# Fused vision-transformer tower on one core: biases as stacked products in PSUM sums, a shorter last norm, gate bias products in four pieces, and a new order on every engine

## The reference, cut to what matters

```python
h = concat([cls_token, patches @ W.T + b]) + pos_enc
# layer 0: norm, gated recurrence over the 37 tokens, residuals; then the feed-forward part
z = sigmoid(norm(x) @ Wg.T + bg); c = norm(x) @ Wc.T + bc      # h_t = (1 - z_t) h_(t-1) + z_t c_t
h = gelu(x @ absmean(W_fc)); h = layernorm(h, ln_w, ln_b) @ absmean(W_proj).T
# layer 1: attention of one head with rotary positions and a causal mask; then a ternary projection
Q, K = rope(x @ Wq.T + bq), rope(x @ Wk.T + bk);  V = x @ Wv.T + bv
A = softmax(where(causal, Q @ K.T / sqrt(256), -inf));  attn = (A @ V) @ Wf.T + bf
y = clip(round(norm(x) / s), -127, 127) @ (ternary_weight - 1).T * s + bias     # s = max(act_scale, 1e-5)
```

## Time and profile before

| what | us |
|---|---|
| median of 3 runs | 170.02 |
| lowest, highest | 169.44, 171.18 |
| the profiled execution's own time | 171.55 |
| its span, first to last instruction | 169.5 |
| PE busy in the span | 151.0 (89%) |
| DVE busy | 128.4 (76%) |
| ACT busy | 96.2 (57%) |
| POOL busy | 93.5 (55%) |

### The profile page before, as it was taken

One profiled execution on the slowest core, in us unless ns is written; L12 is line 12 of the kernel. 1 busy time (PEld: TensorE's weight loads), 2 busy tenths in 40 slices (PEclk: granted clock), 3 DMA queues, 4 the chain that ended last, 5 costly groups with the idle time before them and its releaser, 6 DMA issues.

```text
span 169.5 us, 3258 instructions
## 1 busy us (share of the span) xinstructions
PE 151.0 (89%) x933; PEld 125.1 (74%) x933; DVE 128.4 (76%) x400; ACT 96.2 (57%) x235; POOL 93.5 (55%) x193
## 2 busy tenths in 40 slices
PE   0898999999999899899999999999999996997442
PEld 0668788899997774578987989999988973764231
DVE  0036065979899899799788989879798888648893
ACT  3104087279245798998879669555644461666400
POOL 0001342053521757108986598788778897587850
PEclk9999699999999999999999999999999998799855
DMA  5999991000500000000101011110200000001213
GB/s 183 255 411 420 421 385 52 0 2 0 155 4 0 0 4 0 2 4 0 41 24 31 0 37 31 33 35 0 62 0 0 0 4 0 4 2 31 81 60 118
DMA packets 6614, 12.26 MB, mean 72 GB/s; under 512 B 1061, under 2 KB 4165, under 8 KB 6341
## 3 DMA queue, kind: packets, MB, share of 16 engines
q1 hardware_dynamic: 6597, 12.05, 20.5%
HBM read 9.66 MB, written 1.21 MB: 64 GB/s over the span
## 4 chain that ended last, share of the span: by engine, by line
PE 58%; DVE 12%; POOL 11%; issue 7%; DMA 4%; ACT 3%; SPq 3%; DVEq 0%; POOLq 0%
PE bank L519 30%; PE bank L639 12%; POOL small L1464 5%; DMA w_gate<-w_gate_in 4%; PE bank L711 4%; PE bank L651 3%; PE bank L779 3%; SPq L461 3%; POOL small L1468 2%; DVE q L1430 2%; PE bank L796 1%; PE bank L816 1%; POOL end L1574 1%; POOL small L1459 1%; DVE end L1436 1%
## 5 line engine op out<-in xcount | busy, mean ns | idle before, releaser
L1459 POOL TENSOR_SCALAR small<-small 128x1 f32<-128x1 f32 (+3 forms) x48 | 11.5, 240 | 52.4 <-DVE small L1065 49.8
L639 PE MATMUL bank<-w_tok,x_raw 128*128 128x256 f32 x108 | 29.0, 426 | 5.3 <-DMA w_tok<-w_tok_in 4.9
L1464 POOL TENSOR_TENSOR small<-small,powers 128x1 f32<-128x1 f32 (+4 forms) x48 | 30.9, 645 | 4.7 <-DVE small L1330 1.5
L639 PEld LDWEIGHTS bank<-w_tok,x_raw 128*128 128x128 f32 x108 | 22.6, 216 | 9.0 <-issue 4.9
L519 PE MATMUL bank<-pj,gt_hi 128*128 128x256 f32 x72 | 18.4, 294 | 0.0
L519 PE MATMUL bank<-pj,gt_lo 128*128 128x256 f32 x72 | 17.5, 282 | 0.0
L1384 DVE SCALAR_TENSOR_TENSOR rope<-bank,packed,consts 128x324 f32<-128x324 f32 (+2 forms) x24 | 13.1, 610 | 1.2 <-PE bank L519 1.0
L519 PE MATMUL bank<-fc,n1t_hi 128*128 128x512 f16 x36 | 13.6, 378 | 0.4 <-ACT g L964 0.3
L519 PEld LDWEIGHTS bank<-pj,gt_hi 128*128 128x128 f32 x72 | 13.5, 188 | 0.4
L519 PEld LDWEIGHTS bank<-pj,gt_lo 128*128 128x128 f32 x72 | 13.6, 189 | 0.1
L519 PE MATMUL bank<-fc,n1t_lo 128*128 128x512 f16 x36 | 13.6, 379 | 0.0
(11 more groups left out here) (178 smaller groups left out, 434.8 us busy)
## 6 DMA issues: line engine op xcount, KB each, us to landing
x_raw<-x_in SPq DMA_DIRECT2D x9, 384.0 KB, 7.7
out_dram<-end SPq DMA_DIRECT2D x10, 108.0 KB
w_fc<-w_fc_in SPq DMA_DIRECT2D x1, 1024.0 KB, 9.9
w_pj<-w_pj_in SPq DMA_DIRECT2D x1, 1024.0 KB, 12.7
w_tok<-w_tok_in SPq DMA_DIRECT2D x2, 384.0 KB, 4.1
w_gate<-w_gate_in SPq DMA_DIRECT2D x1, 512.0 KB, 7.4
w_qk<-w_qk_in SPq DMA_DIRECT2D x1, 512.0 KB, 12.5
ln_w<-ln_w_in SPq DMA_DIRECT2D x1, 512.0 KB, 3.7
```

Of the source, the lines that this page charges most:

```text
L639: mm(out[:, 0:D], x_raw[:, i, k, :], w_tok[:, k, :], start=(k == 0), stop=False)
L1459: return nc.gpsimd.tensor_scalar(small[0:n, i, out:out + 1], small[0:n, i, value:value + 1], factor, add, ALU.mult, ALU.add)
L1464: return gt(small[0:n, i, r:r + width], small[0:n, i, ve:ve + width], powers[0:n, 0:width], ALU.pow)
```

## The change

- Keys and values: the class key moves from column 0 of each group's keys to the last, the mask follows (a second mask for the group of 2 images). The transposed probabilities then have the class as their last row, and the class's value is row n of `value`: each `value` sum opens with one product on all 128 rows (a 1 in rows 64 and 96 of `sel`, 0 elsewhere, by `away`, which now holds class value + bias, high and low part) that writes it there. `attend` multiplies n + 1 rows. POOL's 11 `vbias` steps go; DVE's `attend` waits for the DMA of the residual instead.
- `c_value`: DVE adds the bias first (`c_bias`), ACT copies 128 rows, DVE makes two low parts; `c_row` takes one product more, and DVE only copies it.
- Output bias: bias / s, high part in row 0 and low part in row 32 (`w_out_shift`, one ACT and one DVE instruction), enters each `out` sum as a first product on 64 rows, issued ahead of the wait for the copied transposes. POOL's 12 `biased` steps go, and DVE's wait for them.
- Last norm: s squared enters the variance step, so that the power gives 1/(s * deviation) at once; POOL's L1564 goes, and L1459 reads its factor and addend from SBUF in place of constants.
- Gate bias: the same 16 products in four steps `w_gate:0` to `w_gate:3`, in ring `WIDE`.
- DVE's `shift` of the first norm becomes a tensor_scalar with two scalars from SBUF.
- All four lists of `ORDER` are new.

```diff
     "tensor": """
-        tok:0 tok:1 w_gate:0 c_sum:0 tok:2 c_square:0 tok:3 tok:4 w_ternary:0 t0:0 t0:1 tok:5 t0:2 tok:6 tok:7 t0:3
+        tok:0 tok:1 c_sum:0 tok:2 tok:3 w_gate:0 w_gate:1 w_gate:2 w_gate:3 c_square:0 tok:4 w_ternary:0 tok:5 t0:0
...
-        turn:1 value:3 turn:2 attend:1 qk:8 attend:2 qk:9 value:4 qk:10 score:3 score:4 qk:11 turn:3 score:5 t3:1
-        score:6 turn:4 attend:3 value:5 value:6 turn:5 attend:4 turn:6 attend:5 attend:6 score:7 t3:2 score:8
-        score:9 score:10 t3:3 turn:7 value:7 turn:8 value:8 t3:4 attend:7 turn:9 value:9 attend:8 attend:9 turn:10
-        out:0 t3:5 value:10 t3:6 out:1 attend:10 out:2 out:3 t3:7 out:4 t3:8 out:5 t3:9 out:6 t3:10 out:7 out:8
-        out:9 out:10 t3:11 out:11""",
+        score:3 score:4 qk:11 turn:3 score:5 attend:3 score:6 turn:4 t3:1 value:5 turn:5 turn:6 value:6 attend:4
+        attend:5 attend:6 score:7 score:8 t3:2 score:9 score:10 turn:7 t3:3 value:7 value:8 attend:7 turn:8 turn:9
+        value:9 attend:8 attend:9 out:0 turn:10 t3:4 t3:5 value:10 out:1 t3:6 attend:10 out:2 out:3 out:4 out:5 t3:7
+        t3:8 out:6 out:7 out:8 t3:9 out:9 t3:10 out:10 t3:11 out:11""",
     "scalar": """
...
-        turn:7 n3:5 score:9 value:7 score:10 turn:8 value:8 turn:9 t3:4 value:9 n3:6 turn:10 n3:7 t3:5 t3:6 value:10
-        n3:8 n3:9 t3:7 n3:10 t3:8 t3:9 n3:11 t3:10 t3:11""",
+        score:9 value:7 turn:7 value:8 n3:5 turn:8 turn:9 score:10 value:9 n3:6 t3:3 n3:7 turn:10 n3:8 value:10 t3:4
+        t3:5 n3:9 t3:6 t3:7 t3:8 n3:10 n3:11 t3:9 t3:10 t3:11""",
     "vector": """
...
-        sinv:3 score:5 score:6 sbias:5 sinv:4 attend:3 sinv:5 sbias:6 clip:2 rope:5 round:2 sinv:6 stats3:4 attend:4
-        stats3:5 mean3:4 attend:5 attend:6 clip:3 stats3:6 score:7 score:8 round:3 mean3:5 sbias:7 sbias:8 clip:4
-        score:9 sinv:7 stats3:7 mean3:6 score:10 sbias:9 sbias:10 sinv:8 round:4 clip:5 mean3:7 attend:7 round:5
-        stats3:8 attend:8 sinv:9 mean3:8 attend:9 stats3:9 clip:6 mean3:9 round:6 out:0 stats3:10 sinv:10 clip:7
-        mean3:10 round:7 out:1 attend:10 stats3:11 clip:8 out:2 out:3 round:8 clip:9 mean3:11 round:9 clip:10 out:4
-        out:5 round:10 out:6 clip:11 out:7 round:11 out:8 out:9 out:10 out:11""",
+        score:4 sbias:4 round:1 score:5 sbias:5 sinv:3 attend:3 score:6 sbias:6 rope:5 clip:2 sinv:4 sinv:5 stats3:4
+        attend:4 attend:5 sinv:6 stats3:5 attend:6 mean3:4 round:2 mean3:5 clip:3 score:7 sbias:7 score:8 round:3
+        sbias:8 score:9 stats3:6 sbias:9 score:10 mean3:6 stats3:7 sinv:7 clip:4 mean3:7 sinv:8 sbias:10 round:4
+        attend:7 stats3:8 sinv:9 clip:5 sinv:10 round:5 mean3:8 attend:8 clip:6 attend:9 stats3:9 round:6 out:0
+        clip:7 stats3:10 clip:8 mean3:9 out:1 round:7 attend:10 mean3:10 out:2 stats3:11 out:3 out:4 round:8
+        mean3:11 out:5 clip:9 out:6 round:9 clip:10 out:7 round:10 out:8 clip:11 round:11 out:9 out:10 out:11""",
     "gpsimd": """
...
-        vbias:4 proj:5 vbias:5 vbias:6 rope:0 square:7 proj:6 square:8 rope:1 vbias:7 proj:7 proj:8 vbias:8 vbias:9
-        rope:2 attend:1 biased:0 rope:3 vbias:10 attend:2 attend:3 rope:4 biased:1 biased:2 biased:3 rope:5 attend:4
-        attend:5 biased:4 attend:6 attend:7 biased:5 biased:6 attend:8 attend:9 attend:10 attend:11 biased:7
-        biased:8 biased:9 biased:10 biased:11""",
+        rope:1 proj:7 proj:8 rope:2 rope:3 attend:1 attend:2 attend:3 rope:4 rope:5 attend:4 attend:5 attend:6
+        attend:7 attend:8 attend:9 attend:10 attend:11""",
...
@@ value (PE)
+                mm(out[0:n + 1, 0:D], sel[:, SEL_CLASS - n:SEL_CLASS + 1], away[:, :], start=True, stop=False)
-                pairs += [(sel[0:64, SEL_MINUS:SEL_MINUS + n], away[0:64, :])]
@@ out (PE)
+                mm(out[0:n, 0:D], sel[0:64, SEL_BIAS:SEL_BIAS + n], out_shift[0:64, :], start=True, stop=False)
+                pe.wait_ge(s["q3t_ready"], e + 1)
@@ attend (GpSimd)
-                scaled(e, VE3, MV3 + 1, 1.0, LN_EPS, n).then_inc(s["ve3_ready"], 1)
+                if e == 0:
+                    pool.wait_ge(s["scale2_ready"], 2)
+                scaled(e, VE3, MV3 + 1, derived[0:n, D_SCALE2:D_SCALE2 + 1], derived[0:n, D_EPS_SCALE2:D_EPS_SCALE2 + 1], n)\
+                    .then_inc(s["ve3_ready"], 1)
                 pool.wait_ge(s["ve3_ready"], e + 1)
-                power(e, VE3, R3, 1, n).then_inc(s["r3_ready"], 1)
-                if e == 0:
-                    pool.wait_ge(s["inv_scale_ready"], 1)
-
-                pool.wait_ge(s["r3_ready"], e + 1)
-                gt(small[0:n, e, RQ:RQ + 1], small[0:n, e, R3:R3 + 1], derived[0:n, D_INV_SCALE:D_INV_SCALE + 1],
-                   ALU.mult).then_inc(s["rq_ready"], 1)
+                power(e, VE3, RQ, 1, n).then_inc(s["rq_ready"], 1)
-            def biased(e):
-                n = end_rows(e)
-                pool.wait_ge(s["s3_ready"], e + 1)
-                if e == 0:
-                    pool.wait_ge(s["dma_bias"], 16)
-                gt(end[0:n, e, :], end[0:n, e, :], out_bias[0:n, :], ALU.add).then_inc(s["biased_ready"], 1)
@@ out (Vector)
-                dve.wait_ge(s["biased_ready"], e + 1)
```

More of the change, by code:

```diff
@@ L133 @@
-        proj:2 t1:8 c_square:3 tg:6 fc:14 t2:1 tg:7 fc:15 tg:8 fc:16 tg:9 c_value:0 proj:3 c_row:0 tg:10 tg:11 fc:17
-        t2:2 proj:4 tg:12 value:0 tg:13 proj:5 qk:0 tg:14 tg:15 qk:1 t2:3 proj:6 value:1 tg:16 qk:2 t2:4 tg:17 qk:3
-        value:2 proj:7 t2:5 proj:8 score:0 t2:6 qk:4 qk:5 t2:7 qk:6 turn:0 score:1 attend:0 t2:8 score:2 t3:0 qk:7
-        turn:1 value:3 turn:2 attend:1 qk:8 attend:2 qk:9 value:4 qk:10 score:3 score:4 qk:11 turn:3 score:5 t3:1
-        score:6 turn:4 attend:3 value:5 value:6 turn:5 attend:4 turn:6 attend:5 attend:6 score:7 t3:2 score:8
@@ new lines @@
+        fc:16 proj:3 tg:10 tg:11 proj:4 t2:2 fc:17 tg:12 c_row:0 proj:5 tg:13 qk:0 qk:1 tg:14 qk:2 value:0 proj:6
+        tg:15 value:1 tg:16 tg:17 value:2 t2:3 qk:3 t2:4 proj:7 t2:5 proj:8 qk:4 score:0 qk:5 qk:6 turn:0 t2:6
+        score:1 attend:0 t2:7 score:2 t2:8 qk:7 turn:1 value:3 attend:1 qk:8 turn:2 t3:0 attend:2 qk:9 value:4 qk:10
+        score:3 score:4 qk:11 turn:3 score:5 attend:3 score:6 turn:4 t3:1 value:5 turn:5 turn:6 value:6 attend:4
+        attend:5 attend:6 score:7 score:8 t3:2 score:9 score:10 turn:7 t3:3 value:7 value:8 attend:7 turn:8 turn:9
@@ L520, in split_product, with w_gate_bias @@
                 return last
[L522 to L530 removed]
+            def w_gate_bias(b):
+                out = banks[WIDE[("gate_bias", 0)][0]]
+                if b == 0:
+                    pe.wait_ge(s["dma_gate"], 16)
+                    pe.wait_ge(s["dma_packed"], 16)
+                for k in range(KD):
+                    last = mm(out[:, b:b + 1], w_gate[:, k, b * 128:(b + 1) * 128],
+                              packed[:, BETA + k:BETA + k + 1], start=(k == 0), stop=(k == KD - 1))
                 last.then_inc(s["pe_gate_bias"], 1)
@@ L744, in value_ @@
                     pairs += [(hi, wv_hi[:, k, :]), (hi, wv_lo[:, k, :]), (lo, wv_hi[:, k, :])]
-                pairs += [(sel[0:64, SEL_MINUS:SEL_MINUS + n], away[0:64, :])]
-                split_product(out[0:n, 0:D], pairs).then_inc(s["pe_value"], 1)
+                for m_, (a, b) in enumerate(pairs):
+                    last = mm(out[0:n, 0:D], a, b, start=False, stop=(m_ == len(pairs) - 1))
+                last.then_inc(s["pe_value"], 1)
             def qk_(u):
@@ L795, in attend @@
                 pe.wait_ge(s["value_ready"], j + 1)
-                mm(out[0:n, 0:D], pt[0:n, j % 2, 0:n], value[0:n, j, :], start=True, stop=True)\
+                mm(out[0:n, 0:D], pt[0:n + 1, j % 2, 0:n], value[0:n + 1, j, :], start=True, stop=True)\
                     .then_inc(s["pe_attend"], 1)
@@ L880, in c_value, with w_out_shift @@
             def c_value(_i):
-                act.wait_ge(s["cls_tensor"], cls_step("tensor", "value"))
-                go(away[0:64, :], banks[NARROW[("c_value", 0)][0]][0:64, 0:D], ACT.Copy)\
-                    .then_inc(s["cls_scalar"], 1)
+                act.wait_ge(s["cls_vector"], cls_step("vector", "bias"))
+                go(away[:, :], value_bias[:, :], ACT.Copy).then_inc(s["cls_scalar"], 1)
+            def w_out_shift(_i):
+                act.wait_ge(s["dma_bias"], 16)
+                act.wait_ge(s["inv_scale_ready"], 1)
+                act.wait_ge(s["pe_hs"], TILES)
+                go(out_shift[0:64, :], out_bias[0:64, :], ACT.Copy, scale=derived[0:64, D_INV_SCALE:D_INV_SCALE + 1])\
+                    .then_inc(s["out_shift_hi_ready"], 1)
             def h0_(i):
@@ L996, in value_ @@
                 act.wait_ge(s["n0_ready"], min(j + 1, TILES))
-                go(value[0:n, j, :], banks[NARROW[("value", j)][0]][0:n, 0:D], ACT.Copy)\
+                go(value[0:n + 1, j, :], banks[NARROW[("value", j)][0]][0:n + 1, 0:D], ACT.Copy)\
                     .then_inc(s["value_ready"], 1)
@@ L1013, in turn @@
                     act.wait_ge(s["pe_attend"], j - 1)
```

(2 more changed lines are left out.)

201 lines of the change are left out of this document (106 added, 95 removed).

## The result

The changed kernel took 160.26 us (median of 4 executions, 160.08 to 162.15) beside 169.76 us for the kernel before on the same chip: a ratio of 0.945, with a 95% interval of 0.936 to 0.954. The prediction had 163.7 us and 160.5 to 167.8, so the time lies 0.24 us under its low end. The profiled execution of after took 160.11 us with a span of 158.1, where that of before had 169.5: the spans differ by 11.4 us, the medians by 9.5.

What follows compares the result with a forecast made beforehand. PE was taken to bound 80 to 139 us, with PE and DVE near full before and a chain of waits from 140 us. Gains 0.4 + 1.05 + 0.9 + 4.0 = 6.35 from 170.02 gave 163.7 us, range 160.5 to 167.8.

Steps and rivals of the forecast that it cites:

- A, the start: Start of the kernel: earlier `c_sum:0` and `tok:2`, no slow `tok:2`; gain 2.0 us against the profile, 0.4 against the median.
- B, the values: `value` sums with all products of full height: five ahead of `qk:11` gain 1.25 us, 1.05 after the added `c_row` product.
- C, the last keys: DVE's list around `rope:5`, with `clip:2` put behind it: keys and `score:7` earlier by 0.9 us, bounds 0.2 and 1.4.
- The middle order: New order from 16 to 135 us: no row prices it, taken as 0, bounds -2 and +4 us.
- The eleven value additions: POOL's `vbias` steps, 9.0 us of its work beside a full PE: removing them costed at nothing.
- D, the end: From `score:7` on: 1.2 us from POOL's work, 3.1 from stall and outputs, less 0.3 for 64-row `out` products: 4.0.
- The 0.6 for piled-up outputs: End of the kernel: outputs piled up behind the stalled rounding are done earlier, worth some 0.6 us.
- POOL's time not on the path (1): In the end, removed POOL work returns as waits; only the stall and the value gain are won: 166.5 us, chance 0.15.
- DVE as the bound in the middle (2): Waits on DVE swallow the start, value and key gains; only the end's gain is left: 166.0 us, chance 0.10.
- Middle costs (3): The new middle order costs PE waits of about 5 us and eats the gain: 168.5 to 170 us, chance 0.12.
- The slower rival (4): In the last stretch, 12 64-row `out` products at half clock add 1.0 us each: 175.7 us, chance 0.05.
- The stall stays (5): The end's long DVE rounding waits for something other than POOL and stays: 166.2 us, chance 0.04.

Runs made afterwards that it cites:

- no value additions: The kernel before in the four new lists, its eleven GpSimd value-bias additions left out and the twelve output-bias ones kept: 167.93 us, ratio 0.9858.
- output bias by GpSimd: The changed kernel with the twelve GpSimd output-bias additions brought back in place of the bias product in `out`: 165.91 us, ratio 0.9721.

## Why the prediction was right or wrong

The sum against the profile was 7.95 us, and 11.4 came; against the median it was 6.35, and 9.5 came. The stall, the cheaper values and the earlier keys came as worked out, within 0.4 us each. What failed is that the middle was put at 0, that six of the value sums and the clock behind `score:7` had no term, and that the value additions were put at nothing. By its own steps:

- A, the start: 2.0 against the profile, 1.43 came, all of it the clock (1.68 us by the two executions with the old start; the first step behind `tok:1` began 0.24 us later in after). The order's own 0.4 did not come (the old start with a full clock is level). The reading that the other executions mostly don't have the slow `tok:2` is doubtful: four traces of five have it, so the medians probably gain more than 0.4. No trace shows those other executions themselves.
- B, the values: 1.05 up to `qk:11`, and the run that undoes it has 1.43 there. The sum's time was right (0.82 to 0.92 against a worked 0.92), the number of values on the path too; each cost 0.29 on the mean in place of 0.25. The six others were "counted in the end", but D has no term for them: 1.05 us more.
- C, the last keys: 0.9, and 0.75 came.
- The middle order, put at 0 with a bound of -2, is the step that failed most clearly. The lead grew by 3.1 us from the last `tok` to the last `qk` sum; less the 1.43 of B, 1.7 is the order's. Up to `proj:3`, ahead of every value sum, it was 2.7, so the order gave 1 back behind it. It was not without rows: 1.8 us of PE idle from 40 to 80 us stood in the windows, and 1.2 of them went. This and the value sums of the end alone are more than the 0.24 us by which the time missed the range.
- The eleven value additions, put at nothing for lying beside a full PE: wrong in the new order, where they cost some 3 us, in the places that were chosen for them. The cover was read from the old order, where the code edits together gave nothing; no run takes these additions alone out of the old order, so that they cost nothing there is argued and not shown.
- D, the end: 4.0, and 6.2 came. The stall was right in cause and size (2.5 for the step, 2.7 at `out:7`); that such holds can begin elsewhere once times shift was not seen. The 0.6 for piled-up outputs did not come. Ahead of the stall 3.7 came. Of these the value sums are 1.05, the clock in the scores some 0.9 and the order of the steps there some 0.9. That leaves, as an estimate, 0.8 us for POOL's time, where 1.2 was let through; the two runs that give POOL its work back agree with a small share (behind `score:7` and up to `out:6` the additions cost nothing clear beside the clock, and the norm step's fourth instruction 0.2 up to `out:10`). The clock was not priced: a mean of 0.77 over the 29.5 us from 140 us on the earlier trace rows is more time at the lower level than the last 9.5 us at 0.50 make, and the rest was scores 7 to 10. The 64-row out products were put at 0.3 and cost 0.5 by the spans and 0.8 by the medians.

The rivals. POOL's time not on the path (1): false as to the time, 166.5; but it was half right in the mechanism, since POOL's time without the stall was worth about 0.8 us in the end. DVE as the bound in the middle (2): false; DVE's share went up to 37.44 of 40 us and the lead came all the same. Middle costs (3): the wrong sign. The slower rival (4), 64-row out products at half clock one after the other: false for this kernel, but in the old order the changed code does just this with its last four sums: from `out:7` to the end it takes 1.35 us more than the kernel before. The stall stays (5): false.

What is not settled: why a VectorE clip is held for four additions in some places and for one in another, which of the moved steps in the middle carry its 1.7 us, and what takes the clock down at `score:7`. Of the four traces with GpSimd's output additions three have scores 7 to 10 at half clock (before, no value additions, output bias by GpSimd), of the twelve without them none; but PE's idle time just ahead does not tell them apart: the old code in the new order had 1.02 and 0.75 us of it there and kept full clock.

## What to carry to other kernels

An edit that frees an engine and the order that uses it are one change: here each alone measured nothing (1.0005 and 1.0018) and both together 0.945. So a term "costed at nothing, beside a full engine" holds only for the order in which the cover was read, and a new order wants its own price, from the idle time that it can remove, the slow-clock stretches behind each pause, and the places where a VectorE step that GpSimd can hold begins beside it. A bias product is cheaper on all 128 rows with zeros than on the 64 that hold something, when its neighbours use 128.

## What the runs showed of the hardware that was not expected

- A VectorE clip or rounding that began beside GpSimd instructions end to end was held until the fourth of them ended (four traces: 2.85, 3.09, 2.94, 3.09 us in place of 0.28) or the second of two (four traces: 2.22 and three of 1.82). Others waited for one only (0.70 and 0.58 us). VectorE's output step, which reads PSUM, was not held beside the same additions (0.47 us).
- Behind the same wait of 0.6 us with one-column products around it, TensorE stayed at full clock in one execution (12 products in 2.84 us) and was at the lower level in four others (4.43 to 4.52 us). Behind a wait of 0.75 us ahead of `score:7` it stayed at full clock in after and was at 0.51 in the run with the output bias on GpSimd (1.88 and 3.15 us for the same four sums).
- A product of 64 rows between products of 128 cost 0.29 us up to the next one, and the same product on 128 rows 0.20, though it streams the same 256 columns.
